# Where the mean of a gate matrix is taken: from the main product of one layer to the linear products of the next

## The reference

```python
# layer 0: a 64x64 mix per sequence, then a product with a gated low-rank part
y  = einsum('bct,bcd->bdt', x, L0_cond_weights[itok_B_0_15])
x  = x + (y @ weight.T + lora(y, gates(y)))            # "main product"
# layer 1: one of 8 matrices (1024 x 1024) per sequence, then a ternary feed-forward
z  = einsum('bsi,boi->bso', x, L1_cond_weight[itok_B_3_7])   # "linear products"
def bitlinear(x, w):
    scale = mean(abs(w))
    q = round(clip(w / (scale + EPS), -1.0, 1.0))
    return x @ (q * scale).T
x  = x + bitlinear(bitlinear(z, w_gate) * bitlinear(z, w_up), w_down)
```

## Time and profile before

| | us |
|---|---|
| median of three runs | 1404.03 |
| lowest, highest | 1402.75, 1405.18 |
| the profiled execution | 1402.66 |
| its span, first to last instruction | 1401.0 |
| PE busy in it (matmuls) | 1334.8 (95%) |
| DVE, ACT, POOL busy | 751.2, 370.4, 157.5 |
| mean granted TensorE clock | 0.988 of full |

### The profile page before, as it was taken

The page is one execution under the profiler, slowest core; times in us unless marked ns, Lnnn a source line. Parts: engine busy times, 40 slices in busy tenths (PEclk is TensorE's granted clock), DMA queues, the critical chain, the costliest instruction groups (busy, mean ns, idle before and its releaser), DMA issues.

```text
span 1401.0 us, 24489 instructions
## 1 busy us (share of the span) xinstructions
PE 1334.8 (95%) x8864; PEld 851.6 (61%) x8865; DVE 751.2 (54%) x1159; ACT 370.4 (26%) x401; POOL 157.5 (11%) x115
## 2 busy tenths in 40 slices
PE   5889899979999989999999999999999999999998
PEld 5874444434444444555544688854788844888843
DVE  5467555343355556888855255573355572455521
ACT  3332443100111155777730011120011110111100
POOL 3200000000011000000000023320133210122310
PEclk9999999989999999999999999999999999999999
DMA  8744999979998847999864743353644445543354
GB/s 219 166 122 181 376 410 419 313 240 218 308 252 265 220 146 265 342 337 337 285 231 162 248 141 138 147 219 131 221 155 157 147 184 184 211 157 144 131 202 143
DMA packets 174336, 310.67 MB, mean 222 GB/s; under 512 B 99360, under 2 KB 131360, under 8 KB 166464
## 3 DMA queue, kind: packets, MB, share of 16 engines
q1 hardware_dynamic: 158352, 254.04, 55.6%
q10 hardware_dynamic: 11440, 32.69, 6.3%
q0 software_dynamic: 4480, 23.07, 4.7%
HBM read 220.78 MB, written 68.03 MB: 206 GB/s over the span
## 4 chain that ended last, share of the span: by engine, by line
PE 68%; DMA 9%; DVE 7%; issue 5%; SPq 5%; ACT 4%; POOL 1%; POOLq 0%; ACTq 0%; DVEq 0%
PE pair L982 26%; PE pair L1019 15%; PE pair L854 12%; PE pair L946 6%; DMA region_q<-in_L_cond_weight 5%; PE pair L770 4%; DMA region_q<-wb_scratch 2%; DMA region_w<-in_L_ffn_w_gate 2%; ACT region_q L1202 2%; SPq L474 2%; PE pair L737 1%; PE pair L667 1%; PE pair L725 1%; PE pair L900 1%; DVE region_q L1656 1%
## 5 line engine op out<-in xcount | busy, mean ns | idle before, releaser
L982 PE MATMUL pair<-act_t,region_q 128*128 128x256 f16 x3696 | 404.0, 273 | 0.0
L982 PEld LDWEIGHTS pair<-act_t,region_q 128*128 128x128 f16 x3696 | 361.6, 98 | 42.6 <-issue 0.2
L1019 PE MATMUL pair<-region_q,region_w 128*128 128x512 f16 x1232 | 267.6, 379 | 4.4 <-DMA region_q<-wb_scratch 4.1
L1019 PEld LDWEIGHTS pair<-region_q,region_w 128*128 128x128 f16 x1232 | 120.0, 98 | 150.7 <-DMA region_q<-wb_scratch 5.5
L652 POOL TENSOR_TENSOR region_w<-region_q,region_w 128x1792 f32 (+1 forms) x33 | 118.4, 3589 | 742.7 <-ACT region_w L1239 742.7
L854 PE MATMUL pair<-region_w,act_t 128*128 x816 | 178.9, 379 | 1.8 <-DVE region_q L1566 1.8
L770 PE MATMUL pair<-region_w,act_t 128*128 128x512 f16 x768 | 174.3, 385 | 0.0
L946 PE MATMUL pair<-act_t,region_q 128*128 128x512 f16 x704 | 158.6, 384 | 2.6 <-issue 2.6
L854 PEld LDWEIGHTS pair<-region_w,act_t 128*128 x816 | 79.8, 98 | 94.7 <-issue 2.5
L770 PEld LDWEIGHTS pair<-region_w,act_t 128*128 (+1 forms) x768 | 76.1, 99 | 89.6 <-issue 4.7
L1245 ACT ACTIVATE region_q<-pair 128x512 f32<-128x512 f32 x33 | 19.7, 597 | 402.5 <-PE pair L982 402.5
(11 more groups left out here) (185 smaller groups left out, 1016.8 us busy)
## 6 DMA issues: line engine op xcount, KB each, us to landing
region_q<-wa_scratch SPq DMA_DIRECT2D x33, 1792.0 KB, 7.3
region_q<-wb_scratch SPq DMA_DIRECT2D x28, 1408.0 KB, 6.1
region_q<-in_L_cond_weight SPq DMA_DIRECT2D x40, 512.0 KB, 8.8
w1s_scratch<-region_q ACTq DMA_DIRECT2D x40, 512.0 KB, 8.3
wa_scratch<-region_q SPq DMA_DIRECT2D x22, 896.0 KB, 6.0
region_q<-in_x SPq DMA_DIRECT2D x64, 256.0 KB, 4.8
region_w<-in_L_ffn_w_gate SPq DMA_DIRECT2D x16, 688.0 KB, 5.5
wb_scratch<-region_q SPq DMA_DIRECT2D x11, 896.0 KB, 4.1
```

The costliest lines, as they stand in the source:

```text
L982: mm = pe.matmul(bank(s_bank, b)[:, (1 - h) * HALF:(2 - h) * HALF], ring_a[s][:, h, o_a, k], moving[a], start=(opens and h == 1 and k == 0 ...
L1019: mm = pe.matmul(bank(s_bank, b), iop[:, a, p, o_a, tp * P:(tp + 1) * P], ring_b[r][:, p], start=(opens and p == 0 and a == 0), stop=(not ...
```

## The change

The statistics of w_gate leave the main product. GATE_PIECES and GATE_LOADS go, with the 16 loads of SP and the 16 reductions of DVE. In the linear products w_gate is cut like the others, into 12 pieces of 128x1835. POOL loads one of them per slot ahead of two pieces of w_up or w_down, so three in all, and the loop over k has one turn more: the first one loads two pieces of w_gate and nothing else. Piece k+1 waits until ACT has summed piece k-1. ACT sums a piece behind high_z, by an activation of the function Abs with the accumulator's output. w_up and w_down have four buffers, not six, since w_gate takes two of them; their pieces come one turn of k later, and DVE sums them from slot 3 on and the last six in one group.

```diff
-NPIECE_G = 16
-GATE_PIECES = {10: (0, 1), 11: (2, 3), 12: (4, 5, 6), ...
-GATE_LOADS = {10: (0, 1), 11: (), 12: (2, 3), 13: (4, 5, 6), ...
-NBUF = 6
+NBUF = 4
...
 # SP, main product
                     load_pair(x_nat[s], x_loaded[s], t)
-                    for p in (GATE_LOADS[t] if isinstance(t, int) else ()):
-                        load_gate(p, p % 2, stat_gate)
                     if isinstance(t, int) and t == 12:
                         load_rank(0)
...
-            for p in GATE_PIECES[NT - 1]:
-                load_gate(p, p % 2, stat_gate)
             sp.wait_ge(main_done, NT)
...
 # POOL
+            def load_gate(p):
+                n, at_p = piece_size(p), p * PIECE
+                wait_if(pool, gate_summed, p - 1)
+                pool.dma_start(stat_gate[p % 2][:, 0:n], gate_flat[:, at_p:at_p + n]).then_inc(gate_loaded[p % 2], 16)
...
-            for k in range(NPIECE // 2):
+            for k in range(NPIECE // 2 + 1):
                 ahead = field(pool, F_NEXT, k, NADP - 1)
                 pool.wait_ge(w1_loaded, ahead * 16 + 16)
                 pool.tensor_tensor(tick[:, k:k + 1], ones[0:1, 0:1], ones[0:1, 0:1], ALU.mult)
-                if k > 0:
-                    pool.wait_ge(z_done, k)
+                if k == 0:
+                    load_gate(0)
+                    load_gate(1)
+                    continue
+                pool.wait_ge(z_done, k)
...
-                for p in (2 * k, 2 * k + 1):
+                if k + 1 < NPIECE // 2:
+                    load_gate(k + 1)
+                for p in (2 * k - 2, 2 * k - 1):
                     load_piece(p)
...
 # ACT
+            def sum_gate(p):
+                tile = stat_gate[p % 2][:, 0:piece_size(p)]
+                act.wait_ge(gate_loaded[p % 2], 16 * (p // 2) + 16)
+                act.activation(tile, tile, ACT.Abs, accum_out=stat_g[:, p:p + 1]).then_inc(gate_summed, 1)
...
-            with act.Fori(0, NPIECE // 4) as i:
-                layer1(i)
+            for j in range(NPIECE // 2):
+                copy_z(j + 1, (j + 1) % 2)
+                high_z(j)
+                if j > 0:
+                    sum_gate(j - 1)
...
 # DVE
-                for p in GATE_PIECES[t]:
-                    v.wait_ge(gate_loaded[p % 2], 16 * (p // 2) + 16)
-                    v.tensor_reduce(stat_g[:, p:p + 1], stat_gate[p % 2], X, ALU.add,
-                                    apply_absolute_value=True).then_inc(gate_summed, 1)
...
-                if j >= 2:
-                    for p in (2 * j - 4, 2 * j - 3):
+                if j >= 3:
+                    for p in (2 * j - 6, 2 * j - 5):
                         sum_piece(p)
...
-            for p in range(NPIECE - 4, NPIECE):
+            for p in range(NPIECE - 6, NPIECE):
                 sum_piece(p)
+            v.wait_ge(gate_summed, NPIECE // 2)
+            v.tensor_reduce(ssum[:, 0:1], stat_g[:, :], X, ALU.add).then_inc(stat_summed, 1)
             v.wait_ge(stat_done, NPIECE)
```

More of the change, by code:

```diff
@@ L146, in build_program @@
         z_nat = [view(region_q, 58 + 4 * i, [D], F32) for i in range(2)]
-        stat_in = [view(region_w, 64, [PIECE], F32), view(region_w, 72, [PIECE], F32), view(region_q, 32, [PIECE], F32),
-                   view(region_q, 48, [PIECE], F32), view(region_q, 8, [PIECE], F32), view(region_q, 40, [PIECE], F32)]
-        stat_gate = [view(region_w, 64 + 8 * i, [PIECE_G], F32) for i in range(2)]
+        stat_gate = [view(region_w, 64, [PIECE], F32), view(region_w, 72, [PIECE], F32)]
+        stat_in = [view(region_q, 32, [PIECE], F32), view(region_q, 48, [PIECE], F32), view(region_q, 8, [PIECE], F32),
+                   view(region_q, 40, [PIECE], F32)]
         wq_gate = [view(region_q, 16, [D], F32), view(region_q, 0, [D], F32)]
@@ L181, in build_program @@
         iota = sb("iota", [P, NB], F32)
[L182 removed]
+        stat_g = sb("stat_g", [P, NPIECE // 2], F32)
         stat = sb("stat", [P, NPIECE], F32)
[L184 removed]
+        tick = sb("tick", [1, NPIECE // 2 + 1], F32)
         ssum = sb("ssum", [P, 4], F32)
@@ L626, in _ @@
             flat = [w.rearrange("a b -> (a b)").rearrange("(p n) -> p n", p=P) for w in (w_up, w_down)]
+            gate_flat = w_gate.rearrange("a b -> (a b)").rearrange("(p n) -> p n", p=P)
             def load_piece(p):
@@ L1589, in _ @@
             low_x1(3)
-            with v.Fori(2, 5) as i:
+            with v.Fori(2, NT // 2) as i:
                 for s in range(2):
@@ L1594, in _ @@
                     low_x1(2 * i + s)
-            for t in range(10, NT):
-                residual(t, t % 2, pair[t % 2])
-                for p in GATE_PIECES[t]:
-                    v.wait_ge(gate_loaded[p % 2], 16 * (p // 2) + 16)
-                    v.tensor_reduce(stat_g[:, p:p + 1], stat_gate[p % 2], X, ALU.add,
-                                    apply_absolute_value=True).then_inc(gate_summed, 1)
-                prep_low(t // 2, t)
-                low_x1(t)
-            v.wait_ge(gate_summed, NPIECE_G)
-            v.tensor_reduce(ssum[:, 0:1], stat_g[:, :], X, ALU.add).then_inc(stat_summed, 1)
             def copy_z(k, s):
```

20 lines of the change are left out of this document (3 added, 17 removed).

## The result

The changed kernel took 1473.73 us (median of four runs, 1469.88 to 1477.55), against 1403.39 for the kernel before on the same chip (1401.38 to 1405.18): a ratio of 1.049, 95% interval 1.0471 to 1.0509. The forecast was 1402.0, with 1408.5 as the upper end. It was wrong by 72 us. The profiled execution took 1477.55 us, with a span of 1475.9 and a granted clock of 0.963 (before: 1401.0 and 0.988). Two executions further down ran at a low clock from end to end (e4 at 1577.16 us and 0.846, the kernel before at 2004.82 us and 0.657); they are in the medians and not in the ratios.

What follows compares the result with a forecast made beforehand. PE, busy 95% of the span, was taken as the bound, so only its waits and clock count: -10.5 (main product) + 5.8 (tail) + 2.7 (clock) = -2.0 us, from 1404.03 to 1402; range 1396.5 to 1408.5 for 8 in 10.

Steps and rivals of the forecast that it cites:

- Part 1: Main product of layer 0: without w_gate's reductions, 7.46 us idle before tile 13's turn and 3.05 of clock go, together 10.5.
- the 315 that the text had named as a sign of being wrong: Start of the linear products: expected near 312.7 us; a first linear matmul later than 315 would mean the forecast is wrong.
- Part 2, the cost of the instructions: Linear products: ACT's new sum behind high_z takes 1.9 us, hidden in ACT's idle time; DVE still sums two pieces per slot.
- Part 2, the transposing loads: Linear products: six pieces inside rank 2's and rank 4's loads make 34 us each, just in time; cost 0, bound 3 us.
- rival 2: Linear products: rank 2's load misses slot 6, PE stops over 3.5 us, tail still pays; +6.3, 1410 us; chance 0.21.
- transposes half, lets through what has queued up, and then does the other half: Reading of a transposing load in the earlier trace: 290 GB/s, plain loads run in the middle, then 290 again.
- The clock: Clock lost behind the idle time before the mean matmul: 2.7 us, bounds 0 and 3.1.
- Part 3: End of the statistics: six sums, not four, and late pieces 22 and 23 delay the mean matmul 5.8 us, bounds 4.0 to 7.8.
- The rule weighed in part 2: Round robin between DMA queues would bring rank 2 some microseconds ahead of slot 6; set aside because the trace seemed to disagree.

Runs made afterwards that it cites:

- e4: Changed kernel with POOL's tick looking up the rank of slot k+2 instead of slot k, all w_gate loads kept; 1402.82 us, ratio 0.9986.
- g: Kernel before with w_gate's 16 reductions kept in the main product but none at tile 12; 1396.68 us, ratio 0.9953.
- e1: Changed kernel without w_gate's statistics (no loads, no ACT sums, a constant instead); 1458.82 us, 1.04 times the kernel before.
- e5: Kernel before with only its guard weakened: the tick of turn k waits for the rank behind slot k-1's; 1446.65 us, ratio 1.033.
- e10: e6 with one pair of plain loads issued some 14 us into rank 2's transposing load; one run, 1402.62 us.
- e7: e4 with DVE's sums of pieces 16 to 19 in its last loop turn and four, not six, at the end; 1402.52 us, ratio 0.9986.
- e6: e1 (no w_gate statistics) with the guard of e4; 1401.49 us, ratio 0.9973 against the kernel before.
- e11: e6 with one pair of plain loads 3 us and another 14 us into rank 2's transposing load; one run, 1405.96 us.
- e2: Changed kernel with w_gate's loads cut to 128x16 of each piece, waits and order kept; one run, 1429.59 us.
- e12: e6 with two pairs of plain loads both issued 3 to 5 us into rank 2's transposing load; one run, 1404.86 us.
- e8: e1 with POOL issuing a pair of plain loads per slot, whatever transposes; 1481.54 us, ratio 1.0552.
- e9: e1 with a pair of plain loads per slot issued from ACT's queue, whatever transposes; 1471.27 us, ratio 1.0413.

## Why the prediction was wrong, step by step

**Part 1, right.** No idle time before the turn of tile 13, and no slow matmuls behind it. The stage took 9.85 us less (224.35 to 214.5), and 0.7 more was lost at another wait of it (5.39 us idle for 4.70): 10.5, as taken. The first linear matmul came at 315.85 all the same, past the 315 that the text had named as a sign of being wrong, for the 2.5 us ahead of this stage. g has this part alone, and kept 6.6 us of it by its ratio.

**Part 2, the cost of the instructions, right.** ACT's sum in the timeline of after is an activation and the reading of its accumulator, 1.9 us in sum:

```profile
373.48 1.73 ACT L1174 ACTIVATE region_w<-region_w 128x1835 f32<-128x1835 f32 x1
375.10 0.20 ACT L1174 ACTIVATION_READ_ACCUMULATOR region_w<-region_w 128x1 f32 x1
```

**Part 2, the transposing loads: here the prediction failed.** The step was "2.3 us per MB", and from it "22.3 + 5.1 x 2.3 = 34 us" for six pieces inside rank 2's and rank 4's; "Both just in time: I take 0, with 3 us as the bound (the rate's error over 34 us, about a tenth)". They took 71.7 and 59.6. The mistake was the form of the term: a price per MB, whenever the MB come. It was drawn through two rows, rank 1's (a store and the end of one load beside it) and rank 4's (two loads in one batch), and stretched to two batches of three. The table above holds 4.60 MB in 26.8 us (g, all six pieces issued ahead of the transposing load) and 4.49 MB in 98.4 us (e1): the bytes are the wrong variable. In every load of over 33 us more plain loads were issued 10 to 21 us in, behind earlier ones. The text had both facts before it: "the second batch of three loads (tau 48.6 to 50) is issued before the first is through" stands in rival 2, and the order of POOL showed w_gate's load and its pieces moved by a turn of k while the index of the tick stood still. It never asked what the tick was for. In the kernel before it does not protect the pieces, it protects the transposing load: e5 weakens it by one and loses 3.3%.

**Where the two halves come from.** The text read the earlier trace rows as a load that "transposes half, lets through what has queued up, and then does the other half", and took from it that plain loads wait at a fixed point. The trace doesn't say so. The two loads of the earlier trace rows were issued at 452.58; the DMA view of before at 452.6 to 457.0 us has no packet of theirs (q1 is the transposing load), and the one at 458.2 to 461.2 us has both queues served one for one:

```profile
q1 hardware_dynamic: 4986, 1.28, 127.5%
...
q0 software_dynamic: 102, 0.70, 62.3%
q1 hardware_dynamic: 101, 0.03, 11.1%
```

The first packet came 4.5 us after the issue. With no transposing load about it comes after 1.3 us (418.56 in before); inside one it came after 4.50 to 4.55 us, in all 17 batches of these runs that found POOL's queue empty 3 to 18 us in; only e10's pair, which came as the load ended, waited 1.6 us. So the plain loads set the time of the break by when they are issued, and a second batch makes a second break. That could be read before the run, and it leaves no fixed order that keeps the second part of a transposing load clean.

**Rival 2 had the place and not the size.** PE did stop before slot 6; the price was 37.5 us there where it had said 3.5 to 5.9, and slots 11 and 14 and the turns followed. The chance of 0.21 for a slower kernel was too small for a term that was carried, from two rows with about half the load, to twice as many pieces.

**The clock** fell as said behind stops, but over 71 us of them: 0.85 in this stage, 9.5 us of busy time more, where 2.7 stood in the sum.

**Part 3, right where it could be seen.** In the changed kernel it is hidden, since the tail is behind rank 4's stop. In e4 PE stands 7.24 us before the mean, 6.6 more than before (forecast 5.8, bounds 4.0 to 7.8), and the turn behind it took 1.94 (forecast 1.97). The steps are those of the forecast too: the six sums begin at tau 160.2, piece 22 goes out at tau 163.0 (forecast 162.3), the last sum ends at tau 174.8 (forecast 174). The whole is -2.0 us of before by its ratio, with an interval of -4.1 to 0; that this is the forecast's sum to a tenth is partly luck, since e4 has another guard. e7 adds that taking two sums out of the group doesn't shorten it.

**The rule weighed in part 2.** The text read the rows so that a transposing load keeps its engines with plain loads waiting, and set the rule of the Trainium skill ("DMA: Bandwidth & Descriptors", Queues, rings and completion order: round robin, packet by packet, between the queue rows with work) aside for that. The DMA view of after at 495 to 525 us, in the stretch behind the issue of rank 4's load, has both queues served one for one:

```profile
q0 software_dynamic: 1773, 11.61, 95.1%
q1 hardware_dynamic: 1770, 0.45, 7.4%
```

1773 plain packets and 1770 of 256 bytes: here the trace agrees with the rule, if its packets are those of the page, and dismissing it was an error; the rows of before had it one for one as well. A transposing load that shares so gets a sixteenth of its pace (0.45 MB in 30 us, against 4.19 MB in 17.4 alone). That is most of the loss at rank 4. Fifteen pieces (14.09 MB), held up by the stops before it, and ACT's three loads went by in the 49 us after its issue, and the rest then took 10.6 us at 290 GB/s (540.6 to 551.2):

```profile
q1 hardware_dynamic: 10653, 2.72, 121.9%
```

Here bytes do count; the forecast's fault was to have six pieces inside. At ranks 2 and 3 it is another thing. At 441 to 476 us, inside rank 3's load:

```profile
DMA packets 4297, 2.21 MB, mean 63 GB/s; under 512 B 4140, under 2 KB 4140, under 8 KB 4296
q1 hardware_dynamic: 4124, 1.06, 103.6%
q0 software_dynamic: 172, 1.15, 21.7%
```

24 transposing packets for one plain one, and still 63 GB/s: the transposing packets themselves have become slow (1.06 MB fill 16 engines for 35 us, where 4.19 MB take 17.4 alone). The rule doesn't tell of that.

**What stays open.** That plain loads meeting the transposing loads make the loss is shown both ways (e4 and e6 take it away, e5 makes it). Why a transposing packet is so much slower once a second batch has joined is not shown by any run here: the traces have the packets' times, not what goes on in the engines. Nor is the size of the loss: two batches of two make 37.4 us in e11, 40.8 and 98.4 in e1 (there the four came one by one, and behind rank 4's three loads of ACT followed), and in e2 rank 3 took only 33.1 us with four pieces early and two late, whose first packets found a quarter of it still to do. So a second batch was there in every collapse, and is not enough for one. That lateness decides, and not the batch ahead, is not excluded: no run has a single batch of loads that meets a transposing load late with much of it left.

## What to carry to other kernels

A wait that looks superfluous may protect a transfer, not the data behind it: when loads move by one turn of a loop, move the index of such a guard too, and list which plain loads fall inside each transposing load, and in how many batches. A DMA rate read from rows with one batch must not be stretched to two: a transposing load takes 17 us here alone, 17 to 29 with plain loads ahead of it or one batch issued in its first 9 us, 30 to 104 when another batch comes behind those. And where a gap comes from one badly placed reduction, moving the reduction by a tile (g, two tables of numbers) gained 6.6 us, while moving the whole work to another stage gained next to nothing at its best (e4, 0.1%).

## What the runs showed of the hardware

- A transposing load of 4.19 MB runs at 290 GB/s and takes 17.4 us alone. One batch of four plain loads at 3 to 5 us makes 29.4 of it (e12). With a second batch behind the first the rate of all 16 engines fell to 36 to 143 GB/s at a DMA share of about 1 (rank 2's load in the changed kernel, 50 us long), but not each time (e2's rank 3). It didn't matter whether the plain loads came by POOL's or by ACT's queue (e8, e9).
- The first packet of a plain load of POOL came 1.3 us after its issue (before, 418.56 us), and 4.5 us after it when a transposing load was under way (before, 452.58 us). From then on the two shared the engines packet by packet, one for one.
- The time of such a kernel can scatter: e1's four runs span 80 us, the same kernel with the guard of e4 (e6) 6 us in ten. The changed kernel's own four runs span only 8 us, so a narrow spread is no sign that nothing meets.
- An ACT activation of 128x1835 with the accumulator's output takes 1.73 us and 0.20 us more for an instruction that reads the accumulator.
